# Value products in runs of two steps, and the softmax sums inverted on a compact tile, in a fused attention and expert kernel

## The chip, the cores and the metric

One Trainium2 chip, one of its cores. The metric is the device time of the whole program in microseconds (us), median of several runs. The text names TensorE (PE in the rows), VectorE (DVE), ScalarE (ACT), GpSimd (POOL) and SyncE (SP, which here only issues transfers).

## The reference

Sixteen items, each a row of 1101 tokens (1024 image patches and 77 text tokens) with 128 features, go through an embedding, a normalisation, one attention layer with 8 heads of 64, a residual, a second normalisation and a small mixture of experts. What the change touches is the attention:

```
scores = jnp.einsum('bhsk,bhtk->bhst', q, k) / jnp.sqrt(jnp.asarray(K, x.dtype))
probs = jax.nn.softmax(scores, axis=-1)
o = jnp.einsum('bhst,bhtk->bhsk', probs, v)
concated = jnp.transpose(o, (0, 2, 1, 3)).reshape(B, S, H * K)
return jnp.einsum('bse,ed->bsd', concated, head_kernel)
```

All data is float32, and the outputs too.

## The kernel before, in words

An item is cut into 108 **steps**: 4 pairs of heads, times 3 chunks of 368 (the last 366) query columns, times 9 key tiles of 128 (the last 77) rows. A step s is (p, c, t), and the nine steps of one (p, c) are here called a block; q counts the blocks of an item from 0 to 11. In step s:

- TensorE makes the scores of both heads of the pair, transposed, keys by queries, two matmuls a head (`score`, L759 and L761), into three rotating PSUM banks (`SB = 3`).
- ScalarE takes the exponential of each (L867) into one of three buffers of `probs` (`NP = 3`, buffer s % 3). The row maximum that keeps it in range was put into an extra row of the queries beforehand, by transfers (`maxrow`, L1200 and L1202).
- GpSimd adds the probabilities up over the nine key tiles into `sums` (L1151 and L1155), two buffers, one for even and one for odd blocks.
- TensorE multiplies the values of step s - 1 with their probabilities (`weigh`, L778) into the one bank `o_ps`, accumulated over the nine steps of a block. Each head uses 64 columns of the array, head 0 the lower, head 1 the upper half. The profile shows a float32 product as two records, so one call of `weigh` is four records of L778.

After a block: ScalarE copies `o_ps` into `heads_t` (L855). Two steps into the next block, TensorE sums `sums` over the partitions with a matrix of ones, in two halves of 64 columns again (the unit `sum`, L686), ScalarE copies that out (L826), VectorE inverts it in four pieces of 92 columns (`divide`, L991), one piece a step, and multiplies `heads_t` with it in the fifth (L997).

Between score and weigh of a step, and behind weigh, TensorE does **units** of other work, which go through four PSUM banks called `work`: projections of the next pair (`qk`, L669), the values (`v`, L662), raw scores of which VectorE takes the row maximum (`max`, L675, reduced by L925), and the experts of the item before (L718, L723, L734). A function `plan` decides ahead which unit stands in which step: by a table of loads (tens of ns on TensorE, VectorE, ScalarE), it puts some at fixed steps and fills the rest so that the steps are evenly loaded. Half of a step's units stand ahead of `weigh`, half behind. All engines run the same list of steps in order, so what an engine waits for holds up everything behind it in its own list. Items 1 to 14 are a loop on the chip; item 0 and item 15 are written out; the experts of item 15 follow as an epilogue without attention.

The two lines that set ScalarE's pace beside the scores are

```
wait(act, probs_used, ALL * b + s - NP + 1)
wait(act, sums_done, (NT - 1) * PAIRS * NC * b + summed(s - NP))
```

that is, a buffer of `probs` is written again when TensorE has weighed it and GpSimd has added it.

## Time and profile before

| | |
|---|---|
| median of 3 runs | 5209.72 us (5208.44 to 5212.94) |
| span of the profiled execution | 5214.6 us |
| busy share: TensorE matmul | 95% |
| busy share: VectorE | 73% |
| busy share: ScalarE | 51% |
| busy share: GpSimd | 54% |
| mean granted TensorE clock | 0.980 |
| length of one item in the loop | 318.10 us (from 1961.33 to 2279.43) |

The profiled execution is given by its span, which is 4.9 us (0.1%) over the median of the runs. Matmul records overlap: a record of 0.33 us follows the one before at a distance of 0.17 us, so it is the distance between starts, not the busy share, that says what a matmul costs.

### The profile page before, as it was taken

What the parts mean: (1) busy time and instruction counts of PE and PEld (TensorE: products, weight loads), DVE (VectorE), ACT (ScalarE), POOL (GpSimd) and SP (SyncE); (2) the same over time, 40 slices, a digit from 0 to 9 for tenths busy, and PEclk for the clock granted to TensorE, in tenths of its full rate; (3) what the DMA queues carried; (4) which work ended last, traced back from release to release, by engine and by line L of the source; (5) the groups of instructions that cost most, each with busy time, mean ns of one, the idle gap of its engine ahead of it and who ended that gap; (6) DMA issues with size and microseconds to landing.
All of it is one profiled execution on the core that took longest, in us unless ns stands there. A gap on an engine that the chain in (4) does not pass through costs nothing. (4 is left out here: it accounts for less than half of the span.)

```text
span 5214.6 us, 92843 instructions
## 1 busy us (share of the span) xinstructions
PE 4965.0 (95%) x25829; PEld 3227.2 (62%) x25829; DVE 3832.6 (73%) x8495; ACT 2665.8 (51%) x6408; POOL 2796.0 (54%) x1611
## 2 busy tenths in 40 slices
PE   5999999999999999999999999999999999999997
PEld 3556666666566666666666666666666656666666
DVE  5667768677776777777777776777867777677765
ACT  2664555555544545545455455455455554554542
POOL 0665555555555555555555555555555555555652
PEclk7999999999999999999999999999999999999998
DMA  1000000000000000000000000000000000000000
GB/s 39 6 10 7 6 16 6 11 7 6 16 6 10 7 10 11 6 11 11 10 6 6 10 11 11 7 6 16 6 11 7 6 16 6 10 6 10 6 1 14
DMA packets 43025, 49.54 MB, mean 10 GB/s; under 512 B 26256, under 2 KB 34311, under 8 KB 42503
## 3 DMA queue, kind: packets, MB, share of 16 engines
q1 hardware_dynamic: 42503, 43.12, 2.7%
q8 instruction: 262, 4.29, 0.4%
q14 instruction: 260, 2.13, 0.1%
HBM read 23.45 MB, written 19.09 MB: 8 GB/s over the span
## 5 line engine op out<-in xcount | busy, mean ns | idle before, releaser
L1155 POOL TENSOR_TENSOR sums<-sums,probs 128x736 f32<-128x736 f32 (+3 forms) x1344 | 2384.6, 1774 | 1278.0 <-ACT probs L867 1262.6
L867 ACT ACTIVATE probs<-scores 128x368 f32<-128x368 f32 (+3 forms) x3456 | 1460.1, 474 | 1922.0 <-PE scores L761 1814.5
L925 DVE TENSOR_REDUCE part_max<-work 128x1 f32<-128x368 f32 (+3 forms) x3456 | 1657.3, 527 | 310.1 <-PE work L675 288.3
L778 PE MATMUL o_ps<-probs,values 128*64 128x368 f32 (+1 forms) x6912 | 1455.7, 500 | 0.0
L759 PE MATMUL scores<-q_a,k_a 128*128 128x368 f32 (+3 forms) x3456 | 1170.2, 339 | 61.1 <-issue 41.5
L761 PE MATMUL scores<-q_b,k_b 128*128 128x368 f32 (+3 forms) x3456 | 1146.4, 332 | 0.0
L675 PE MATMUL work<-k_a,q_a 128*128 128x368 f32 (+3 forms) x3456 | 1089.6, 378 | 48.0 <-DVE part_max L925 24.4
L675 PEld LDWEIGHTS work<-k_a,q_a 128*128 128x128 f32 (+1 forms) x3456 | 578.3, 184 | 777.4 <-issue 624.1
L1151 POOL TENSOR_TENSOR sums<-probs 128x736 f32<-128x736 f32 (+1 forms) x192 | 343.6, 1789 | 863.5 <-ACT probs L867 861.5
L759 PEld LDWEIGHTS scores<-q_a,k_a 128*128 128x128 f32 (+1 forms) x3456 | 639.5, 185 | 83.8 <-issue 33.2
L761 PEld LDWEIGHTS scores<-q_b,k_b 128*128 128x128 f32 (+1 forms) x3456 | 641.3, 186 | 53.0 <-issue 33.7
L778 PEld LDWEIGHTS o_ps<-probs,values 128*64 128x64 f32 (+1 forms) x6912 | 349.5, 135 | 412.6 <-issue 327.3
L969 DVE SCALAR_TENSOR_TENSOR h_out<-work,comb,h_out 128x128 f32<-128x128 f32 x1152 | 404.1, 351 | 268.1 <-PE work L734 236.0
L991 DVE RECIPROCAL sums<-sums 128x92 f32<-128x92 f32 (+1 forms) x768 | 543.1, 713 | 12.8 <-ACT sums L826 11.7
L915 DVE TENSOR_TENSOR k_b<-work,k_a 64x368 fp32r<-64x368 f32 (+1 forms) x384 | 204.5, 533 | 375.8 <-ACT k_a L822 373.9
L918 DVE TENSOR_TENSOR q_a<-work,q_b 64x368 fp32r<-64x368 f32 (+1 forms) x384 | 207.0, 539 | 158.5 <-ACT q_b L822 153.2
L734 PE MATMUL work<-down_hi,hid_hi 128*128 128x512 f32 x576 | 237.6, 413 | 0.4 <-DVE q_a L918 0.4
L734 PE MATMUL work<-down_hi,hid_lo 128*128 128x512 f32 x576 | 231.0, 401 | 0.0
L734 PE MATMUL work<-down_lo,hid_hi 128*128 128x512 f32 x576 | 230.8, 401 | 0.0
L813 ACT COPY values<-work 128x256 f32<-128x256 f32 x288 | 107.6, 374 | 206.0 <-PE work L662 205.6
L820 ACT CAST k_a<-work 64x368 fp32r<-64x368 f32 (+1 forms) x384 | 177.2, 461 | 36.8 <-PE work L669 31.1
L820 ACT CAST q_a<-work 64x368 fp32r<-64x368 f32 (+1 forms) x384 | 176.2, 459 | 29.3 <-PE work L669 24.4
(186 smaller groups left out, 5039.6 us busy)
## 6 DMA issues: line engine op xcount, KB each, us to landing
resid_rows<-h_in SPq DMA_DIRECT2D x16, 576.0 KB, 2.8
h_out<-resid_rows SPq DMA_DIRECT2D x16, 576.0 KB, 4.1
h_in<-in_pe_table_dram SPq DMA_DIRECT2D x16, 512.0 KB
out_dram<-h_out SPq DMA_DIRECT2D x16, 512.0 KB
q_b<-max_rows SPq DMA_DIRECT2D x128, 4.0 KB
q_b<-max_rows SPq DMA_DIRECT2D x128, 0.3 KB
counts<-in_x_dram SPq DMA_DIRECT2D x16, 116.0 KB, 3.0
out_raw<-n_expert_out_weight_dram SPq DMA_DIRECT2D x1, 1024.0 KB
```

Of the source, the lines that this page charges most:

```text
L675: mm = nc.tensor.matmul(w[0:n, 0:cw], q_a[p % 2][i][:, j * P:j * P + n], k_a[p % 2][i][:, c0:c0 + cw], start=True, stop=True)
L734: mm = nc.tensor.matmul(w, h[:, k2, cols], wt[:, k2, g * EG * D:(g + 1) * EG * D], start=(n == 0), stop=(n == len(ops) - 1))
L759: nc.tensor.matmul(o, k_a[p % 2][i][:, t * P:t * P + n], q_a[p % 2][i][:, c0:c0 + cw], start=True, stop=False)
L761: nc.tensor.matmul(o, k_b[p % 2][i][:, t * P:t * P + n], q_b[p % 2][i][:, c0:c0 + cw], start=False, stop=True).then_inc(scores_ready, 1)
L778: mm = nc.tensor.matmul(o_ps[64 * i:64 * i + 64, 0:cw], values[0:n, t, h * DH:(h + 1) * DH], probs[0:n, s % NP, i, 0:cw], start=(t == 0), ...
L820: nc.scalar.copy(a[p % 2][i][0:64, c0:c0 + cw], src)
L867: nc.scalar.activation(probs[0:n, s % NP, i, 0:cw], scores[0:n, h % SB, 0:cw], ACT.Exp, scale=DH ** -0.5).then_inc(probs_ready, 1)
L925: nc.vector.tensor_reduce(part_max[0:n, i * NT + j, c:c + 1], w[0:n, 0:keys], AX.X, ALU.max).then_inc(drained[k], 1)
L969: ins = nc.vector.scalar_tensor_tensor(out=o, in0=w[:, e * D:(e + 1) * D], scalar=comb[:, t, g * EG + e:g * EG + e + 1], in1=o, op0=ALU.mu ...
L991: nc.vector.reciprocal(inverse[:, cols], inverse[:, cols]).then_inc(s_chain, 1)
L1151: nc.gpsimd.tensor_tensor(acc, probs[:, (s - 1) % NP, :, 0:cw], probs[:, s % NP, :, 0:cw], ALU.add).then_inc(sums_done, 1)
L1155: nc.gpsimd.tensor_tensor(acc, acc, probs[0:n, s % NP, :, 0:cw], ALU.add).then_inc(sums_done, 1)
```

## The change

Five things.

1. `weigh` is called in bursts. The nine steps of a block are grouped 2, 2, 2, 2, 1; the products of a group stand in the step behind it, so at t = 2, 4, 6, 8 (two steps each) and at t = 0 of the next block (the one left over). Steps t = 1, 3, 5, 7 have none.
2. `probs` keeps three buffers with another rule: the first step of a group takes buffer 0 or 1 in turn, the second always buffer 2. ScalarE's two waits go by that rule (`held`).
3. The unit `sum` stands in the step t = 2 as before (in the last block's case at step 2 of the next item, before at step 1), now directly behind the burst.
4. The inverse: the row of sums of each head goes by two transfers from one partition into a compact tile `inv_cols` of 92 partitions by 8 columns; VectorE inverts that in one instruction two steps after the sum; one transfer stores it to DRAM and two bring it back, each spread over 64 partitions.
5. GpSimd multiplies `heads_t` with it, at t = 0 of the second block after (step 0 and step 7 of the next item for the last two blocks).

The planner's loads change with it (a step 66 for the scores, and in a step with a burst 25 more and 62 for each product), so other units move too.

```
+GROUPS = (2, 2, 2, 2, 1)
+MOST = max(GROUPS)
+NP = 2 * MOST - 1
+SUM_AT = 2
+INVERT, SCALE_LAST = 2, 7
+RW = 8
-STEP = (130, 0, 70)
+SCORE = (66, 0, 70)
+EXCURSION, WEIGH = 25, 62
...
+def slot(s):
+    n, _, _, position = group_of(s)
+    return n % 2 * (MOST - 1) + position if position < MOST - 1 else NP - 1
...
+def held(s):
+    return next(back for back in range(1, ALL) if slot((s - back) % ALL) == slot(s))
...
         def step(seg, it, b, s):
             if seg.attn:
                 p, c, t = cut(s)
-                wait(act, probs_used, ALL * b + s - NP + 1)
-                if not isinstance(b, int) or b > 0 or s >= NP:
-                    wait(act, sums_done, (NT - 1) * PAIRS * NC * b + summed(s - NP))
+                back = held(s)
+                wait(act, probs_used, ALL * b + s - back + 1)
+                if not isinstance(b, int) or b > 0 or s >= back:
+                    wait(act, sums_done, (NT - 1) * PAIRS * NC * b + summed(s - back))
...
+        def invert(b, q):
+            dve.wait_ge(cols_loaded, 32 * (item_of(b, q) + 1))
+            nc.vector.reciprocal(inv_cols[:], inv_cols[:]).then_inc(cols_inverted, 1)
...
+        def scale(b, q):
+            c0, cw = CHUNKS[q % NC]
+            o = heads_t[:, q // NC, c0:c0 + cw]
+            pool.wait_ge(inverse_loaded[q % 2], 32 * (PAIRS * NC // 2 * b + q // 2 + 1))
+            pool.wait_ge(heads_out, PAIRS * NC * b + q + 1)
+            nc.gpsimd.tensor_tensor(o, sums[:, q % 2, 0, 0:cw], o, ALU.mult).then_inc(heads_scaled, 1)
...
+                elif u[0] == "sum":
+                    wait_then(wait_drained, sp, seg, it, u)
+                    for i in range(2):
+                        row = sums[64 * i:64 * i + 1, u[1] % 2, 0, :]
+                        half = slice(i * CHUNK // RW, (i + 1) * CHUNK // RW)
+                        sp.dma_start(inv_cols[half, :], row.rearrange("p (a n) -> p a n", n=RW)).then_inc(cols_loaded, 16)
+            for u in seg.at[s - INVERT] if s >= INVERT else []:
+                if u[0] == "sum":
+                    n = item_of(b, u[1])
+                    wait_then(sp.wait_ge, cols_inverted, n + 1)
+                    sp.dma_start(inv_dram[u[1] % 2].rearrange("(a n) -> a n", n=RW), inv_cols[:]).then_inc(cols_stored, 16)
+                    wait_then(sp.wait_ge, cols_stored, 16 * (n + 1))
+                    for i in range(2):
+                        row = inv_dram[u[1] % 2:u[1] % 2 + 1, i * CHUNK:(i + 1) * CHUNK]
+                        sp.dma_start(sums[64 * i:64 * i + 64, u[1] % 2, 0, :], row.broadcast_to((DH, CHUNK))).then_inc(inverse_loaded[u[1] % 2], 16)
```

TensorE, in a quiet stretch of the loop (block 1 of the item, the step t = 6 of the kernel before, from its second head's scores): a step is the scores, a unit, the products of the step before, more units. `ISA` and `REGISTER_ALU` rows hold waits and their arithmetic; `x2` stands for the two heads.

```order
L598 REGISTER_ALU
L759 MATMUL scores<-q_a,k_a 128x368
L761 MATMUL scores<-q_b,k_b 128x368
L598 REGISTER_ALU
L675 MATMUL work<-k_a,q_a 128x366
L767 ISA
L778 MATMUL o_ps<-probs,values 64x368 x2
L598 REGISTER_ALU
L675 MATMUL work<-k_a,q_a 128x366 x2
L598 REGISTER_ALU
```

The same engine and block in the changed kernel, the step t = 6 (L813 and L815 are the scores, L729 the raw scores for the maxima, L832 the products):

```order
L813 MATMUL scores<-q_a,k_a 128x368
L815 MATMUL scores<-q_b,k_b 128x368
L648 REGISTER_ALU
L729 MATMUL work<-k_a,q_a 128x366
L821 ISA
L832 MATMUL o_ps<-probs,values 64x368 x2
L821 ISA
L832 MATMUL o_ps<-probs,values 64x368 x2
L729 MATMUL work<-k_a,q_a 128x366
L729 MATMUL work<-k_a,q_a 128x368
```

Two products now stand side by side, and the step ahead of this one has none. Over the loop body, the runs of matmuls in 64-column halves (products and sums, counted as one run where nothing full-width stands between) are 117 before and 60 after; in the item ahead of the loop 115 and 59, in the last item with its epilogue 114 and 60.

TensorE before, where a block's sum stands (L686, block 1 of the item): full-width work (L695, L675) stands between it and the products.

```order
L759 MATMUL scores<-q_a,k_a 128x368
L761 MATMUL scores<-q_b,k_b 128x368
L598 REGISTER_ALU
L683 REGISTER_ALU
L686 MATMUL work<-sums,ones 64x368 x2
L695 MATMUL work<-wo,heads_t 128x128 x4
L675 MATMUL work<-k_a,q_a 128x368
L767 ISA
L778 MATMUL o_ps<-probs,values 64x368 x2
```

TensorE after, such a place at the loop's start (L740 is the sum): it is the tail of the burst.

```order
L821 ISA
L648 REGISTER_ALU x2
L832 MATMUL o_ps<-probs,values 64x368 x2
L821 ISA
L832 MATMUL o_ps<-probs,values 64x368 x2
L737 ISA
L740 MATMUL work<-sums,ones 64x366 x2
```

So the sum opens no run of its own any more, in any block.

The queue of SyncE before, around the first `maxrow` of the loop, which stands three steps behind the sum of block 1 and four ahead of the pair that needs it:

```order
L598 ISA
L1200 DMA q_b<-max_rows 1x8x128
L1202 DMA q_b<-max_rows 1x13x6
L1200 DMA q_b<-max_rows 1x8x128
L1202 DMA q_b<-max_rows 1x13x6
L598 ISA
```

The queue of SyncE after, the same place (L1259 and L1261 are the `maxrow` transfers; ahead of L1272 it waits for VectorE's inverse, ahead of L1276 for the store to have landed):

```order
L1267 DMA inv_cols<-sums 46x1x8 x2
L1228 REGISTER_ALU
L1272 DMA inverse_rows<-inv_cols 92x8
L1228 REGISTER_ALU
L1276 DMA sums<-inverse_rows 64x368 x2
L648 REGISTER_ALU
L1259 DMA q_b<-max_rows 1x8x128
L1261 DMA q_b<-max_rows 1x13x6
L1259 DMA q_b<-max_rows 1x8x128
L1261 DMA q_b<-max_rows 1x13x6
```

The `maxrow` transfers now queue behind a store, the wait for it, and two loads.

## Rows read from the trace of the kernel before

**Rows 1.** The page: span, busy times and shares.

```profile
span 5214.6 us, 92843 instructions
PE 4965.0 (95%) x25829; PEld 3227.2 (62%) x25829; DVE 3832.6 (73%) x8495; ACT 2665.8 (51%) x6408; POOL 2796.0 (54%) x1611
```

**Rows 2.** Windows, an item: length, busy PE, PEld, DVE, ACT, POOL (instructions), clock, DMA, GB/s.

```profile
1961.33:2279.43 318.10, 306.76 (x1609) 199.31 (x1610) 238.66 (x525) 165.98 (x399) 174.34 (x100) 0.99 0.03 9
```

**Rows 3.** Timeline of TensorE: start us, length us, engine, line, count.

```profile
2007.72 0.33 PE L761 MATMUL scores<-q_b,k_b 128*128 128x368 f32 x1
2007.89 0.33 PE L675 MATMUL work<-k_a,q_a 128*128 128x366 f32 x1
2008.15 0.84 PE L778 MATMUL o_ps<-probs,values 128*64 128x368 f32 x4
2008.92 0.44 PE L675 MATMUL work<-k_a,q_a 128*128 128x366 f32 x1
2009.20 0.33 PE L759 MATMUL scores<-q_a,k_a 128*128 128x368 f32 x1
```

**Rows 4.** Timeline of TensorE where a sum and a product stand together.

```profile
2365.81 0.84 PE L686 MATMUL work<-sums,ones 128*64 128x366 f32 x4
2366.48 0.79 PE L778 MATMUL o_ps<-probs,values 128*64 128x368 f32 x4
2367.20 0.43 PE L669 MATMUL work<-yt_hi,wqk_hi 128*128 128x368 f32 x1
2367.47 0.33 PE L669 MATMUL work<-yt_lo,wqk_hi 128*128 128x368 f32 x1
```

**Rows 5.** Groups by line: busy us, mean ns, idle before and releasers.

```profile
L867 ACT ACTIVATE probs<-scores 128x368 f32<-128x368 f32 (+3 forms) x3456 | 1460.1, 474 | 1922.0 <-PE scores L761 1814.5 <-POOL sums L1155 72.1 <-issue 24.4
L1155 POOL TENSOR_TENSOR sums<-sums,probs 128x736 f32<-128x736 f32 (+3 forms) x1344 | 2384.6, 1774 | 1278.0 <-ACT probs L867 1262.6
L991 DVE RECIPROCAL sums<-sums 128x92 f32<-128x92 f32 (+1 forms) x768 | 543.1, 713 | 12.8 <-ACT sums L826 11.7
L1062 DVE RECIPROCAL den<-den 128x9 f32<-128x9 f32 x16 | 3.4, 215 | 0.6
L997 DVE TENSOR_TENSOR heads_t<-sums,heads_t 128x368 f32<-128x368 f32 (+1 forms) x192 | 182.2, 949 | 3.8
L820 ACT CAST k_a<-work 64x368 fp32r<-64x368 f32 (+1 forms) x384 | 177.2, 461 | 36.8 <-PE work L669 31.1
```

**Rows 6.** Timeline: the queue of SyncE, and the scores of the next pair.

```profile
2352.08 0.68 SPq L1200 DMA_DIRECT2D q_b<-max_rows  x1
...
2354.35 0.77 SPq L1202 DMA_DIRECT2D q_b<-max_rows  x1
2357.83 0.33 PE L759 MATMUL scores<-q_a,k_a 128*128 128x368 f32 x1
```

**Rows 7.** Timeline, and the page's list of transfers (KB, us to landing).

```profile
117.54 0.77 SPq L1202 DMA_DIRECT2D q_b<-max_rows  x1
119.41 0.68 PE L759 MATMUL scores<-q_a,k_a 128*128 128x368 f32 x1 [4.08 <-DMA q_b<-max_rows]
...
resid_rows<-h_in SPq DMA_DIRECT2D x16, 576.0 KB, 2.8
```

**Rows 8.** Timeline around GpSimd's root in step 13.

```profile
2009.50 1.81 POOL L1130 TENSOR_TENSOR rstd<-var,minus_half 128x9 f32<-128x9 f32 x1 [3.49 <-DVE var L1024]
...
2013.43 0.85 ACT L867 ACTIVATE probs<-scores 128x368 f32<-128x368 f32 x2 [2.85 <-POOL sums L1155]
```

**Rows 9.** Timeline: the start of an item in the loop.

```profile
2281.40 0.48 ACT L867 ACTIVATE probs<-scores 128x368 f32<-128x368 f32 x1 [3.71 <-issue]
```

**Rows 10.** Timeline of the epilogue's sum and scaling.

```profile
5122.25 0.84 PE L686 MATMUL work<-sums,ones 128*64 128x366 f32 x4 [2.52 <-POOL sums L1155]
5127.84 0.53 DVE L997 TENSOR_TENSOR heads_t<-sums,heads_t 128x366 f32<-128x366 f32 x1
```

**Rows 11.** Timeline: a multiplication on VectorE while GpSimd adds.

```profile
2273.93 1.96 DVE L997 TENSOR_TENSOR heads_t<-sums,heads_t 128x368 f32<-128x368 f32 x1
```

More of the change, by code:

```diff
@@ L106, in maxima, with group_of, burst @@
     return units, first_need
+def group_of(s):
+    t, start = s % NT, s - s % NT
+    for n, size in enumerate(GROUPS):
+        if t < size:
+            return s // NT * len(GROUPS) + n, start, size, t
+        t, start = t - size, start + size
+def burst(s):
+    _, start, _, position = group_of((s - 1) % ALL)
+    if position < group_of((s - 1) % ALL)[2] - 1:
+        return []
+    start -= ALL if s == 0 else 0
+    return list(range(start, s))
+def slot(s):
[3 more added lines that the diff above has]
+    return next(back for back in range(1, ALL) if slot((s - back) % ALL) == slot(s))
 def load(u):
@@ L114, in plan @@
     at = [[] for _ in range(ALL)]
-    used = [list(STEP) if attn else [0, 0, 0] for _ in range(ALL)]
+    used = [list(SCORE) if attn else [0, 0, 0] for _ in range(ALL)]
+    for s in range(ALL):
+        if attn and burst(s):
+            used[s][0] += EXCURSION + WEIGH * len(burst(s))
     def job(s, name):
@@ L199, in plan, with beside_weighing @@
         fill(units, WEIGHTS + 3, STORE - 2, EVEN_POST)
-    return at
+    return [beside_weighing(units) for units in at]
+def beside_weighing(units):
+    sums = [u for u in units if u[0] == "sum"]
+    others = [u for u in units if u[0] != "sum"]
+    n = len(units) // 2
+    return others[:n] + sums + others[n:]
 class Segment:
```

71 lines of the change are left out of this document (33 added, 38 removed).

## The prediction

> **What bounds the kernel now.** The busy shares come first: TensorE 95%, no other engine over 73% [rows 1]. That share is no proof, since matmul records overlap, so I read starts. In the timeline a full-width matmul of 368 columns follows the one before at 0.17 us (2007.72 to 2007.89) [rows 3]. I priced the list of one item in the loop that way, from such distances: 216 each of L759, L761 and L675, 72 of L669 at 0.166 us (119.5); L718, L734 and L662 at 0.174, 0.232 and 0.117 (43.9); smaller units 18.9; the 64-column matmuls as below (120 products and sums at 0.615, 117 runs at 0.357: 115.5 with rounding). The sum is 297.7 us, and an item takes 318.1 [rows 2]. So TensorE streams for 94% of the loop, and about 20 us an item are waits and half-clock stretches. A shorter list on TensorE shortens the program, as long as nobody else comes to set the pace.
>
> The groups by line say the same from the other side: ScalarE waited 1814.5 us for scores and only 72.1 for GpSimd's sums; GpSimd 1262.6 for ScalarE [rows 5].
>
> **What a run in half-width columns costs.** The last full-width matmul before the products starts at 2007.89, the products at 2008.15: 0.26 where 0.17 is usual. The next full-width one starts 0.77 later (2008.92), and its successor 0.28 after that [rows 3]. So a run of one product takes 0.26 + 0.77 + 0.28 less two usual distances of 0.17, 0.98 us. Where a sum and a product stand together, both go in 1.39 (2365.81 to 2367.20), and the successor follows at 0.27 [rows 4]; the gap ahead is again 0.26, and there are 62 such places after scores, nearly all alike. The second member adds 0.62 where a run of its own adds 0.98: each run that goes away gives back 0.36 us (0.357 by the middle values of all such places: 0.154 inside, 0.095 ahead, 0.108 behind).
>
> The Trainium skill says in "TensorEngine Tiling (Array Packing)", section Key Properties, that changing the tiling mode, not just the tile, drains TensorE. By that rule too the price hangs on the number of changes of width, and the trace agrees with its 0.26 and 0.28 at the two edges.
>
> **The change, part by part.**
>
> *Bursts and sums.* Runs in the loop fall from 117 to 60 an item, in the first item from 115 to 59, in the last with epilogue from 114 to 60: 57 x 14 + 56 + 54 = 908. At 0.357 that is 324 us. The products themselves stay (0.62 each). That two products in a row cost what a sum and a product do is not shown: they add into the same bank `o_ps`, the sum goes to another. Bounds: 0 if a product behind a product costs 0.98 again, 0.36 if like the sum. Inside one product its own two passes already add to one bank without harm (four records in 0.77), so I take 0.36.
>
> *VectorE.* 768 pieces at 0.713 and 192 multiplications at 0.949 go, 725 us; 192 compact inverses come. No row has 92 x 8, the nearest is 128 x 9 at 0.215: 0.2 each, 40 us. TensorE waits for VectorE now and then, a gain of 0 to 2 us an item; I take 1.
>
> *GpSimd.* 192 multiplications of 368 columns; the nearest row is 1.774 us for 736, so between 0.9 and 1.8; I take 0.9. A block then costs it 8 x 1.77 + 0.9 = 15.1 us, TensorE's block (297.7 - 20.3) / 12 = 23.1. Hidden; the shortest pair of steps in the new plan is 3.4 us on TensorE against 3.5 for two additions, which is no lasting lag.
>
> *The chain of the inverse.* Copy of the sums 0.5 (a cast of the same width takes 0.46 [rows 5]), two issues 1.4, landing, VectorE 0.2, store issue 0.7, landing, two load issues 1.4, landing. An issue takes 0.66 to 0.79 [rows 6]. A landing is 1.1 us after the issue's end for a small transfer (118.31 to 119.41), and 2.8 after the issue of a large one [rows 7]. That makes 4.2 + 3 x 1.1 to 3 x 2.1, 7.5 to 10.5 us, plus what VectorE comes late. GpSimd asks for it six steps later, some 15 us. Hidden. VectorE asks for the tile after two steps, at least 3.9 us by the plan, and it lands 3.0 to 4.0 after the sum: hidden or nearly; behind a late one stand VectorE's maxima, which free TensorE's banks. I give 0.5 us an item. [...]
>
> *The queue of SyncE.* Here a wait can come. The inverse of block 1's sum is asked for at step 22, and `maxrow` stands at step 23. It queues behind store issue 0.7, landing 2, load issues 1.4, then needs its own 2.9 [rows 6] and 1.1 to 1.8 to land: about 9.2 us after step 22. TensorE is at the next pair after the four steps 23 to 26, 8.1 us in the new plan. Before, the slack was 2357.83 - 2355.12 = 2.7 less the landing [rows 6]. I charge 1.5 us for this pair and 1 for the start of the item, where the store of the output also stands in the queue; the other two pairs have 10 us and more ahead of them.
>
> *Two buffers back.* The second step of a group now needs the buffer of the step two back, not three. It bites where GpSimd is late. In step 13 it waited 3.49 us for the variance, took 1.81 for the root, and ScalarE's next exponential but two came 2.85 us late [rows 8], without a stop of TensorE. In the new plan the exponential of step 16 needs one addition more (1.77), while TensorE needs it in the same burst: 1.5 us an item.
>
> *ScalarE in the first six steps of a pair.* It has exponentials of 0.85 and four casts of 0.46 a step there [rows 5], 17.7 to 20.7 us, and TensorE before 15.6 to 17.7, after 14.4 to 16.5. What TensorE gains there is partly given back: 1 us an item. The start of an item, where ScalarE comes 3.71 us late and TensorE waits for it [rows 9], stays.
>
> *Epilogue.* The scaling ended 6.1 us after the sum started (5122.25 to 5128.37) [rows 10], under projections that don't need it. The new chain is some 11 us with GpSimd's 0.9, and nothing covers the rest: 5 us.
>
> *Sum.* 324 - 16 x (0.5 + 2.5 + 1.5 + 1 - 1 for VectorE's relief), 72 us, - 5 = 247. From the span of 5214.6 that is 4968, and less the 4.9 us by which the span lies over the median, 4963. I say 4963.
>
> **The rivals.**
>
> *All of it arrives* (0.15). New waits are swallowed by the 20 us an item that TensorE idles anyhow, and VectorE's relief takes more of them away: 5210 - 324, 4886, give or take 12. For it: VectorE drops from 239 to about 196 busy us an item. Against it: the idle stretches lie at the item's start and at pauses, not where the new waits fall.
>
> *Pacing eats half* (0.20). ScalarE, GpSimd and the transfers share three buffers with less slack, and uneven steps (by the same prices 1.2 us for the shortest without a burst, up to 4 with one) leave TensorE waiting once a block: 12 x 0.8 = 10 us an item more, 5120. For it: rows 8 show how near the edge one late addition is. Against: a pair of steps is long enough for one exponential, one addition and one exponential (0.85 + 1.77 + 0.85 = 3.5 against 3.4 at the shortest, 5.1 on average).
>
> *VectorE is held up by GpSimd.* A multiplication of 0.53 alone [rows 10] took 1.96 while additions ran [rows 11]. More work on GpSimd, more such holds; but the one instruction of this kind that came every block is the one that goes away, so this stays inside the forecast. The Trainium skill ("SBUF — State Buffer", section on the two separate sides) calls this an exclusive lock on a shared port pair, held for a whole instruction; the 1.96 agrees. By that rule 0.9 us more a block could stop VectorE, 11 us an item of an engine that then idles some 100.
>
> *Slower* (0.04). The chain of the inverse is longer than the six steps until GpSimd asks. GpSimd then stops ahead of the additions, those hold the buffers, and TensorE stops. It bites from 15 us of chain and costs 192 us per us beyond; from 16.3 us it has eaten the gain, at 19 us the time is 4963 + 192 x 4 = 5731. It would take transfers of 4 to 5 us each; none in the trace needs more than 2.8.
>
> *The change doesn't do it* (0.06). A product behind a product drains as before: only the 60-odd sums that join are gained (9 an item, 144 x 0.36 = 52 us), against 77 of new waits: 5235. That counts as slower; with lighter waits it is within 0.2%.
>
> **The numbers.** Forecast 0.55, all 0.15, half 0.20, nothing 0.06, slower 0.04. Gains over 0.2% (10 us, about what a measurement of this kernel can tell from no change): 0.55 + 0.15 + 0.20 = 0.90, and a little of the fifth: 0.91; same 0.03; slower 0.06. The range holds the forecast with the bounds of its waits (1.5 to 9 us an item: 4915 to 5040), the upper half of the first rival and part of the second: 4890 to 5070.
>
> **What would show it.** Right: 57 runs in half width less in an item, an item of 302 us, products of a burst 0.62 us apart, GpSimd's multiplication at 0.9 with no wait ahead of it, and small waits of TensorE at the start of pair 1 (for `max_rows`) and in step 17. Wrong: products 0.98 apart; GpSimd waiting for `inverse_rows`; VectorE waiting for `inv_cols` by more than a us a block; ScalarE's wait for `sums` far over 72 us with TensorE idle behind it.

## The result, and the profile after

The changed kernel takes 5268.99 us (median of 4 runs, 5256.67 to 5274.85), the kernel before in the same session 5210.89 (5208.44 to 5212.94): a ratio of 1.0107, 95% interval 1.0092 to 1.0121. It is 1.1% slower, 306 us from the forecast, outside its range, and on the side that had 0.06.

The head of the page of the changed kernel, against [rows 1]:

```profile
span 5262.3 us, 94506 instructions
PE 4774.0 (91%) x25829; PEld 3366.3 (64%) x25829; DVE 3256.8 (62%) x7727; ACT 2673.5 (51%) x6408; POOL 2950.3 (56%) x1803
```

TensorE has 191 us less to do and VectorE 576, and the program is 48 us longer. The time saved came back as idle time, and more. The mechanism that was to save is there. Timeline of TensorE in a quiet stretch, a burst with a sum and a burst alone (against [rows 3, 4]):

```profile
2331.26 0.41 PE L729 MATMUL work<-k_a,q_a 128*128 128x368 f32 x1
2331.60 1.46 PE L832 MATMUL o_ps<-probs,values 128*64 128x368 f32 x8
2332.89 0.79 PE L740 MATMUL work<-sums,ones 128*64 128x368 f32 x4
2333.61 0.60 PE L729 MATMUL work<-k_a,q_a 128*128 128x368 f32 x2
...
2336.93 0.33 PE L815 MATMUL scores<-q_b,k_b 128*128 128x368 f32 x1
2337.20 1.46 PE L832 MATMUL o_ps<-probs,values 128*64 128x368 f32 x8
2338.58 0.44 PE L813 MATMUL scores<-q_a,k_a 128*128 128x368 f32 x1
2338.86 0.33 PE L815 MATMUL scores<-q_b,k_b 128*128 128x368 f32 x1
```

Two products take 1.38 (2337.20 to 2338.58), as a sum and a product did in [rows 4]; with the sum it is 2.01 (2331.60 to 2333.61). The gap ahead is still 0.27, the one behind 0.28. A second product costs 0.62 and no second pair of gaps.

The groups by line, against [rows 5], and VectorE's compact inverse and GpSimd's multiplication:

```profile
L927 ACT ACTIVATE probs<-scores 128x368 f32<-128x368 f32 (+3 forms) x3456 | 1462.7, 474 | 1869.5 <-PE scores L815 1649.8 <-POOL sums L1214 182.2 <-POOL sums L1210 24.6
L1043 DVE RECIPROCAL inv_cols<-inv_cols 92x8 f32<-92x8 f32 x192 | 36.4, 190 | 7.3 <-DMA inv_cols<-sums 5.4
L1185 POOL TENSOR_TENSOR heads_t<-sums,heads_t 128x368 f32<-128x368 f32 (+1 forms) x192 | 190.6, 992 | 11.2 <-DMA sums<-inverse_rows 10.9
```

The instructions of the inverse path wait for next to nothing: 5.4 us for `inv_cols` and 10.9 for `inverse_rows` in the whole program (8.2 of it once, in the epilogue). The transfers as such are hidden.

The item, against [rows 2]: 324.14 us, where it had 319.72 at the same place of the program (the eighth item). Windows of that item, the six steps of each pair in which the next pair's projections (`qk`) are made: length, busy PE, PEld, DVE, ACT, POOL, clock, DMA, GB/s. The kernel before:

```profile
2279.43:2300.57 21.14, 18.15 (x89) 11.94 (x90) 8.31 (x16) 14.59 (x34) 7.25 (x6) 0.84 0.01 2
2357.83:2377.62 19.79, 17.64 (x95) 12.10 (x94) 14.40 (x34) 17.34 (x42) 8.44 (x6) 1.00 0.15 36
2442.86:2461.85 18.99, 18.97 (x102) 13.10 (x101) 15.31 (x29) 15.80 (x38) 9.65 (x6) 1.00 0.00 1
2521.82:2541.22 19.40, 18.71 (x101) 12.85 (x100) 12.77 (x25) 17.90 (x44) 8.55 (x5) 1.00 0.00 1
```

The changed kernel:

```profile
2292.36:2315.64 23.28, 18.41 (x88) 13.19 (x89) 7.85 (x17) 14.47 (x34) 8.16 (x6) 0.78 0.07 24
2372.86:2397.34 24.48, 18.22 (x95) 13.25 (x95) 13.92 (x29) 18.89 (x45) 10.55 (x7) 0.95 0.14 35
2457.47:2478.11 20.64, 18.28 (x92) 13.27 (x92) 13.89 (x26) 14.99 (x37) 8.05 (x6) 0.92 0.01 1
2536.66:2561.77 25.11, 20.17 (x102) 14.93 (x101) 12.46 (x25) 18.27 (x43) 9.68 (x6) 0.93 0.02 7
```

The 24 projection steps grew from 79.3 to 93.5 us; the other 84 shrank from 240.4 (2279.43 to 2599.15, less 79.3) to 230.6 (2292.36 to 2616.50, less 93.5). In the second and fourth window TensorE and ScalarE are each idle for 5 to 7 us, so it is no engine's amount of work that makes them long: they wait for each other. The chain of who waits for whom is in TensorE's list of waits (us in total, times, longest), of the changed kernel:

```profile
PE work L772 <- DVE q_a L977: 78.2, 42, 2.2
PE scores L813 <- DMA q_b<-max_rows: 47.7, 30, 4.1
PE work L729 <- DVE k_b L974: 35.0, 32, 1.9
PE work L723 <- DVE q_a L977: 26.2, 30, 1.0
PE work L788 <- DVE q_a L977: 25.5, 25, 1.6
```

The largest, 42 times, is three times an item in 14 items of the loop: in steps 30, 32 and 82. Of the wait in the last row, at L788 (`expert`), 21.9 us are in step 86. L772 is the unit `up` of the experts. It does not read `q_a`: it waits for the bank of `work` that VectorE empties when it makes `q_a`. The plan says why it is those steps. Units of some projection steps, before and now:

```
         before                     changed
step 30  qk max up                  qk max max up up
step 32  qk up                      qk max max up up
step 57  qk max max                 qk max max shared expert
step 82  qk up up                   qk v v up up
step 86  qk expert                  qk max max shared expert
```

There are four banks, and they go round. A fifth unit in a step needs the bank that the `qk` of the same step has just filled. Timeline of step 82 (weight loads and other rows left out):

```profile
2539.99 0.33 PE L723 MATMUL work<-yt_hi,wqk_hi 128*128 128x368 f32 x1
...
2541.52 0.38 PE L716 MATMUL work<-wv_hi,yt_hi 128*128 128x256 f32 x1 [0.51 <-DVE k_b L974]
2541.70 0.85 ACT L927 ACTIVATE probs<-scores 128x368 f32<-128x368 f32 x2
...
2542.10 0.44 PE L772 MATMUL work<-flat_hi,up_hi 128*128 128x384 f32 x1
...
2542.42 0.45 ACT L879 CAST q_a<-work 64x368 fp32r<-64x368 f32 x1
...
2543.63 0.46 ACT L881 CAST q_b<-work 64x368 fp32r<-64x368 f32 x1
...
2544.12 0.54 DVE L977 TENSOR_TENSOR q_a<-work,q_b 64x368 fp32r<-64x368 f32 x1 [0.32 <-ACT q_b L881]
...
2544.72 0.45 PE L772 MATMUL work<-flat_hi,up_hi 128*128 128x384 f32 x1 [1.83 <-DVE q_a L977]
...
2545.57 0.51 PE L813 MATMUL scores<-q_a,k_a 128*128 128x368 f32 x1
...
2545.80 0.49 ACT L899 ACTIVATE hid<-work 128x384 f32<-128x384 f32 x1 [1.04 <-PE work L772]
2545.87 0.51 PE L815 MATMUL scores<-q_b,k_b 128*128 128x368 f32 x1
```

The `qk` of the step starts at 2539.99. Behind it in ScalarE's list stand the two exponentials (2541.70), then four casts of 0.46 from that bank (2542.42 to 2544.09), and behind them VectorE's subtraction (to 2544.66). Only then may the fifth unit start (2544.72), and the next step's scores stand behind it (2545.57): 6.2 us for a step, with ScalarE idle for 1.04 us at its end.

Step 57 also has five units, but loses its time at the third. There the second `max` needs the bank of the `qk` of step 56, and VectorE comes late to empty it, because a cast ahead of it in its list takes 1.96 us while GpSimd adds (the same cast takes 0.35 in step 35):

```profile
2465.56 1.96 DVE L1048 CAST flat_hi<-normed 128x384 fp32r<-128x384 f32 x1
2469.17 0.43 PE L729 MATMUL work<-k_a,q_a 128*128 128x368 f32 x1 [1.86 <-DVE k_b L974]
```

This wait comes to 27.1 us in the program. The kernel before has none of it, though its `max` needs the same bank and the cast takes 1.67 us in the same step; the steps around it hold other units. The fifth unit of step 57 waits 3.6 us in all, those of 30, 32, 82 and 86 together 100.1.

### The profile page after: what moved, and what is told of

It reads as the page before. It is cut to its first block, busy times and chain, and to the rows that moved or that the text cites. A ratio compares the mean times of both kernels' runs of the same rounds, so it can differ in the third digit from the quotient of the medians.

```text
span 5262.3 us, 94506 instructions
## 1 busy us (share of the span) xinstructions
PE 4774.0 (91%) x25829; PEld 3366.3 (64%) x25829; DVE 3256.8 (62%) x7727; ACT 2673.5 (51%) x6408; POOL 2950.3 (56%) x1803
## 4 chain that ended last, share of the span: by engine, by line
PE 69%; ACT 10%; DVE 7%; issue 7%; DMA 2%; SPq 2%; POOL 2%; ACTq 0%; DVEq 0%; POOLq 0%
PE o_ps L832 20%; PE work L729 11%; PE scores L813 8%; PE work L788 8%; PE scores L815 8%; PE work L772 3%; PE work L723 3%; ACT probs L927 2%; DVE part_max L984 2%; PE work L749 2%; ACT q_b L881 2%; ACT q_a L879 2%; PE work L740 2%; ACT k_a L881 1%; ACT k_a L879 1%
## 5 line engine op out<-in xcount | busy, mean ns | idle before, releaser
L984 DVE TENSOR_REDUCE part_max<-work 128x1 f32<-128x368 f32 (+3 forms) x3456 | 1676.7, 532 | 581.3 <-PE work L729 566.4
L832 PE MATMUL o_ps<-probs,values 128*64 128x368 f32 (+1 forms) x6912 | 1304.7, 494 | 0.0
L813 PE MATMUL scores<-q_a,k_a 128*128 128x368 f32 (+3 forms) x3456 | 1186.8, 343 | 82.2 <-DMA q_b<-max_rows 47.7
L815 PE MATMUL scores<-q_b,k_b 128*128 128x368 f32 (+3 forms) x3456 | 1161.3, 336 | 45.1 <-issue 45.1
L729 PE MATMUL work<-k_a,q_a 128*128 128x368 f32 (+3 forms) x3456 | 990.3, 364 | 73.5 <-DVE k_b L974 35.0
L729 PEld LDWEIGHTS work<-k_a,q_a 128*128 128x128 f32 (+1 forms) x3456 | 578.3, 185 | 482.5 <-issue 344.4
L813 PEld LDWEIGHTS scores<-q_a,k_a 128*128 128x128 f32 (+1 forms) x3456 | 651.0, 188 | 217.8 <-issue 114.0
L832 PEld LDWEIGHTS o_ps<-probs,values 128*64 128x64 f32 (+1 forms) x6912 | 416.9, 138 | 498.4 <-issue 409.2
L815 PEld LDWEIGHTS scores<-q_b,k_b 128*128 128x128 f32 (+1 forms) x3456 | 651.1, 188 | 69.0 <-issue 49.2
L788 PE MATMUL work<-down_hi,hid_hi 128*128 128x512 f32 x576 | 245.3, 426 | 32.7 <-DVE q_a L977 25.5
L772 PE MATMUL work<-flat_hi,up_hi 128*128 128x384 f32 x384 | 146.6, 382 | 102.5 <-DVE q_a L977 78.2
L885 ACT COPY sums<-work 128x368 f32<-128x368 f32 (+1 forms) x192 | 89.6, 467 | 283.3 <-PE work L740 280.6
L788 PE MATMUL work<-down_hi,hid_lo 128*128 128x512 f32 x576 | 232.3, 403 | 0.0
L788 PE MATMUL work<-down_lo,hid_hi 128*128 128x512 f32 x576 | 232.2, 403 | 0.0
L1185 POOL TENSOR_TENSOR heads_t<-sums,heads_t 128x368 f32<-128x368 f32 (+1 forms) x192 | 190.6, 992 | 11.2 <-DMA sums<-inverse_rows 10.9
```

The lines of the kernel that those rows point to most:

```text
L729: mm = nc.tensor.matmul(w[0:n, 0:cw], q_a[p % 2][i][:, j * P:j * P + n], k_a[p % 2][i][:, c0:c0 + cw], start=True, stop=True)
L772: mm = nc.tensor.matmul(w[:, 0:GW], wt[:, path, m, :], y[:], start=(n == 0), stop=(n == 2))
L788: mm = nc.tensor.matmul(w, h[:, k2, cols], wt[:, k2, g * EG * D:(g + 1) * EG * D], start=(n == 0), stop=(n == len(ops) - 1))
L813: nc.tensor.matmul(o, k_a[p % 2][i][:, t * P:t * P + n], q_a[p % 2][i][:, c0:c0 + cw], start=True, stop=False)
L815: nc.tensor.matmul(o, k_b[p % 2][i][:, t * P:t * P + n], q_b[p % 2][i][:, c0:c0 + cw], start=False, stop=True).then_inc(scores_ready, 1)
L832: mm = nc.tensor.matmul(o_ps[64 * i:64 * i + 64, 0:cw], values[0:n, t, h * DH:(h + 1) * DH], probs[0:n, slot(s), i, 0:cw], start=(t == 0), ...
```

## The experiments

All against the kernel before in the same session (5209.25 to 5213.72). The last two columns name the projection steps of an item with five and with four units.

| kernel | median us | ratio, 95% interval | five | four |
|---|---|---|---|---|
| changed | 5268.99 | 1.0107 (1.0092 to 1.0121) | 30 32 57 82 86 | 4 28 84 |
| bursts_only | 5175.35 | 0.9923 (0.9905 to 0.9941) | 28 | 32 57 82 |
| inverse_only | 5206.4 | 0.9991 (0.9981 to 1.0001) | none | 4 32 57 59 84 86 |
| max_first | 5245.07 | 1.0066 (1.0045 to 1.0086) | as changed | as changed |
| level | 5104.98 | 0.9791 (0.9774 to 0.9809) | none | 4 32 57 59 84 86 |
| half | 5126.21 | 0.9837 (0.982 to 0.9853) | none | 4 28 30 32 57 59 84 86 |
| level_max | 5085.95 | 0.9764 (0.9747 to 0.978) | none | as level |
| level_old_inverse | 5144.47 | 0.9874 (0.9857 to 0.989) | none | none |
| level_buf4 | 5052.81 | 0.9697 (0.9681 to 0.9713) | none | as level |
| qk_heavy | 5174.43 | 0.9926 (0.991 to 0.9943) | none | 4 32 86 |
| uneven_rest | 5086.32 | 0.9761 (0.9745 to 0.9777) | none | 4 32 57 |
| root_late | 5107.37 | 0.9799 (0.9782 to 0.9815) | none | as level |
| root_qk | 5132.79 | 0.9846 (0.9829 to 0.9862) | none | 4 |
| cap4 | 5180.85 | 0.9935 (0.9918 to 0.9951) | none | 4 28 30 32 57 59 82 84 86 |
| level_five | 5194.97 | 0.9971 (0.9956 to 0.9985) | 32 57 84 86 | 4 |
| rest_max | 5062.52 | 0.9713 (0.9697 to 0.973) | none | 4 32 57 |
| rest_cap3_max | 5046.96 | 0.9682 (0.9666 to 0.9698) | none | none |
| cap3 | 5111.14 | 0.9804 (0.9788 to 0.9821) | none | none |

**Which part of the change?** bursts_only is the changed kernel with the inverse as before, in four pieces on VectorE; inverse_only is the kernel before with the transfers, the compact inverse and GpSimd's multiplication.

```
bursts_only:   -INVERT, SCALE_LAST = 2, 7      +DIV = 4
               -JOB "invert": 8                +JOB "invert": 63, "scale": 45
               -dve: invert(b, u[1])           +dve: divide(seg, it, b, u[1], part)
               -sp: dma inv_cols, inverse_rows, sums;  pool: scale(b, q - 2)
inverse_only:  the same lines the other way round, on the kernel before
(in words; the planner's JOB is VectorE's load of these instructions)
```

> The changed kernel with the inverse as it was before: four reciprocals and a multiplication on VectorE, no transfers, no multiplication on GpSimd. Theory A (the loss comes with the bursts: heavy units pile up in the steps without products, scores get only one step of lead, TensorE and ScalarE take turns in waiting, and the clock drops in the new waits): the time stays near the changed kernel's 5269, between 5230 and 5300, and the waits at steps 30 to 33, 57, 82 and 86 of an item stay. Theory B (the loss comes with the inverse's way over the transfer queue and GpSimd): the 324 us of the fewer runs come through, near 4900 to 4960.

> The kernel before with only the new inverse (compact tile, transfers, multiplication on GpSimd), products one a step, plan by the old loads. Theory A: close to before, 5190 to 5235, with up to 45 us of waits for max_rows as in the changed kernel, and VectorE's relief against it. Theory B: 5400 and more, since the transfers would cost some 380 us with nothing to set against them.

The inverse alone changes nothing that can be measured (5206.4 beside 5212.76). The bursts alone gain 37 us, between what the two theories had (5230 to 5300, and 4900 to 4960). Together they lose. Neither part is at fault alone, and each also moves the planner's units, since both change its loads.

**The planner's table.** level gives every step the same load for scores and products, as before the change; half goes half way.

```
level:  -SCORE = (66, 0, 70)                                          +SCORE = (130, 0, 70)
        -        if attn and burst(s):
        -            used[s][0] += EXCURSION + WEIGH * len(burst(s))
        +        pass
half:   -SCORE = (66, 0, 70)          +SCORE = (98, 0, 70)
        -EXCURSION, WEIGH = 25, 62    +EXCURSION, WEIGH = 12, 31
```

> The changed kernel with the planner's old load of a step (130 in every step, nothing extra for bursts), so units are spread evenly over steps with and without products. Theory A in its form 'uneven units are to blame': the steps without products get shorter and those with products longer, the experts no longer stand ahead of the scores in steps 57, 82 and 86; 5080 to 5200. If it is the bursts themselves that take the lead of the scores away, whatever stands between: 5230 to 5300. Theory B: no change, 5269.

> The changed kernel with a planner's table half way between its own and the flat one: 98 in every step, in a step with a burst 12 more and 31 for each product. If the unevenness of the units is what costs 164 us, the time lies between 5105 and 5269, some 5150 to 5220. If it was one unlucky place of a unit, it lies at one of the two ends.

Three numbers are worth 164 us: 5104.98, 2.1% faster than before. The new table, which follows TensorE's load more closely, is the worse one. Half way gives back nearly all (5126, where 5150 to 5220 was expected), which does not fit a loss in proportion to the unevenness, but fits the number of steps with five units: five in the changed kernel, none in either of these.

**The queue of SyncE.** max_first lets the loads of the inverse go one step later, so that the `max_rows` transfers pass them; level_max does it to level.

```
-                    wait_then(sp.wait_ge, cols_stored, 16 * (n + 1))
+            for u in seg.at[s - INVERT - 1] if s >= INVERT + 1 else []:
+                if u[0] == "sum":
+                    n = item_of(b, u[1])
+                    wait_then(sp.wait_ge, cols_stored, 16 * (n + 1))
```

> The changed kernel, but SyncE brings the inverse back one step later, so that the transfers of max_rows are issued ahead of the wait for the store. TensorE's waits for max_rows (47.7 us over the program against 5.8 before) fall to under 10: 5215 to 5240 by theory A (up to 42 us, and some of the clock). Theory B in its form 'the queue of SyncE is the whole loss': under 5100.

> Flat table and max_rows ahead of the inverse's return, both. If they are separate causes their gains add: 5105 less about 24, 5070 to 5090. If the waits for max_rows only took the place of others: 5105.

Both gain: 24 us and 19. TensorE's wait for `max_rows` falls from 47.7 us in 30 places (41.8 in level) to one at the program's start, so about half of the length of these waits was worth time. In max_first:

```profile
PE scores L813 <- DMA q_b<-max_rows: 4.1, 1, 4.1
```

**Does VectorE's relief pay?** level_old_inverse is bursts_only with level's table (the edits are those shown).

> Flat table, bursts, and the inverse on VectorE as before the change. The transfers cost waits for max_rows (42 us of 5105); VectorE's 700 us of reciprocals and multiplications come back. If the transfers are the greater cost: 5060 to 5090. If VectorE's relief is: 5110 to 5140.

It takes 5144.47, 39 us more than level. So with a flat table the new inverse is a gain, with the new table it comes with a loss of 94 (5175 to 5269), and there it goes with five crowded steps in place of one. Where the old inverse costs most is step 17 of the item, told next: it takes 7.1 us there and 4.6 in level, 39 us over the program. The other steps of the two profiled runs differ both ways: 5.3 us an item less in the projection steps, 6.9 more in the rest.

**The buffers.** level_buf4 is level_max with four buffers of `probs` in plain rotation. To have room it leaves out the low part of the projection weights (`wqk_hi` is used in its place; the matmuls stay).

```
-NP = 2 * MOST - 1      +NP = 4
-    return n % 2 * (MOST - 1) + position if position < MOST - 1 else NP - 1      +    return s % NP
```

> As level_max, with four buffers of probabilities in plain rotation (a step's buffer is free when the step four back is weighed and added) in place of three. To make room it leaves out the low part of the query and key weights (the high part is read twice, same instructions in the loop). If the three buffers with the second step's two-back rule cost time (step 17's 1.7 us an item, and ScalarE's waits for sums): 20 to 50 us under level_max. If not: the same within 10.

33 us less. The run tells time only, since its projections are not the true ones. ScalarE's wait for GpSimd's sums, first in level_max, then in level_buf4:

```profile
ACT probs L926 <- POOL sums L1213: 135.4, 53, 4.2
```

```profile
ACT probs L922 <- POOL sums L1209: 88.6, 46, 2.0
```

The place that loses it is step 17, of 2.4 us before the change, 4.6 in the changed kernel and level_max, and 2.9 in level_buf4. GpSimd waits for the variance, takes the root, and its additions start late behind it; ScalarE needs the buffer that they read, and TensorE the exponential. Timeline of the changed kernel there:

```profile
2339.69 1.81 POOL L1175 TENSOR_TENSOR rstd<-var,minus_half 128x9 f32<-128x9 f32 x1 [2.32 <-DVE var L1070]
...
2341.74 3.58 POOL L1214 TENSOR_TENSOR sums<-sums,probs 128x736 f32<-128x736 f32 x2
...
2345.43 0.85 ACT L927 ACTIVATE probs<-scores 128x368 f32<-128x368 f32 x2 [4.18 <-POOL sums L1214]
2345.96 0.39 PE L813 MATMUL scores<-q_a,k_a 128*77 128x368 f32 x1 [1.49 <-ACT probs L927]
```

root_late tries to cure it without a buffer, and root_qk adds the heavier load of a projection unit that is told next:

```
root_late (on level_max):  -if seg.post and s == STATS:       +if seg.post and s == STATS + 2:
                           -if seg.prep and s == EMBED + 4:   +if seg.prep and s == EMBED + 6:
root_qk (on root_late):    -LOAD "qk": (48, 95, 130)          +LOAD "qk": (112, 95, 130)
```

> The flat table with the transfers of max_rows first (5086), and GpSimd's two roots an item issued two steps later, behind the additions of those steps. If the wait in step 17 comes from the root, which holds the additions while GpSimd waits for the variance, it goes: 1.7 us an item, 27 us, 5060, near the run with four buffers of probs (5053). Rival: the root only moves, and the wait with it, or what hangs on the root comes late: 5080 to 5100.

> As the run before, with the projection unit's load at 112. If lighter projection steps help beside a flat table too, 5040, 20 us less than with 48. Rival: with the flat table there is little left to take there, and the other steps become fuller: within 10 us of the run with 48.

Both were worse than level_max (5107 and 5133 beside 5086). The wait in steps 15 to 17 only fell from 1.8 to 1.2 us an item, and what hangs on the second root came 2.5 us an item later in step 65. Two steps later is too late for the root; no other place was tried. And fewer units in the projection steps are no good by themselves: root_qk is 25 us slower than root_late.

**Where is the table's loss?** qk_heavy keeps the changed kernel's table and makes only projection steps lighter; uneven_rest makes them flat and leaves the new table everywhere else.

```
qk_heavy:     -LOAD "qk": (48, 95, 130)     +LOAD "qk": (112, 95, 130)
uneven_rest:  -        if attn and burst(s):
              +        if attn and s % (NC * NT) < 6:
              +            used[s][0] += 76
              +        elif attn and burst(s):
```

> The changed kernel, only the planner's load of a projection unit (qk) raised from 48 to 112, so that 12 instead of 23 other units of the experts and values stand in its 24 steps of an item; elsewhere the table's alternation of full and empty steps stays. Theory A, the loss sits in the steps of the projections, where heavy units stand between one score and the next behind a bank that ScalarE and VectorE give back late: about 5150, between 5105 (the flat table) and 5180. Rival B, the loss comes from the alternation of steps with and without products wherever it stands: 5240 to 5270, as the changed kernel.

> The mirror of the run with the heavier projection unit: the changed kernel, with the flat load in the six projection steps of each pair (76 added there, nothing for the products), and the new table's alternation in all others. Theory A: most of the gain of the flat table arrives, 5110 to 5150. Rival B: three quarters of the steps still alternate, so 5210 to 5250.

uneven_rest is decisive: with the new table in 84 of 108 steps it takes 5086.32, even less than level. Its 84 other steps take 1.7 us an item more than level's, with two more units in them, and its projection steps 3.1 less. So full and empty steps in turn cost next to nothing outside the projection steps. qk_heavy gains 95 of 164 us: 18 us an item less in the projection steps than the changed kernel, and 12 more in the others, where the units have gone.

**What in those steps?** cap4 and cap3 keep the changed kernel and its whole table and only forbid a fifth (a fourth) unit in a projection step; level_five puts four such fifth units into level.

```
cap4, cap3:  +MAX_UNITS = 4        (cap3: 3)
             +        def full(s, places):
             +            return any(x[0] == "qk" for x in at[s]) and len(at[s]) + sum(n == s for n, _ in places) >= MAX_UNITS
             -                while s <= last and (u == PAUSE or weighted(used[s]) + backlog >= level):
             +                while s <= last and (u == PAUSE or weighted(used[s]) + backlog >= level or full(s, places)):
level_five:  +FIFTH = (32, 57, 84, 86)
             +    for s in FIFTH if post and attn else []:
             +        n = next(n for n in range(s + 1, ALL) if any(u[0] in ("up", "shared", "expert") for u in at[n]))
             +        u = next(u for u in at[n] if u[0] in ("up", "shared", "expert"))
             +        at[n].remove(u)
             +        at[s].append(u)
```

> The changed kernel with its own table of loads; only the planner may not give a projection step a fifth unit, so single units leave the steps 30, 32, 57, 82 and 86 for later ones and nothing else is meant to change. Theory C, the fifth unit of such a step needs the work bank of that step's own qk unit, which stands behind two exponentials, four casts and two subtractions, and holds up the next scores: the waits of the five steps (15.8 us an item in the changed kernel) fall to some 5, 10 us an item, 5090 to 5130. Rival B2, the uneven filling of the projection steps as a whole costs it: it hardly changes there, so 5220 to 5270.

> The mirror: the flat table (5105), and in the steps 32, 57, 84 and 86, which have four units, the next unit of the experts is drawn forward as a fifth; four units an item move by one to three steps. Theory C: each such step costs about 2.5 us more, 10 us an item: 5220 to 5280. Rival B2: four units more or less early cost 0 to 2 us an item: 5100 to 5140.

> The changed kernel and its table, with at most three units in a projection step, so that it has no fourth either (the cap of four gave 5181). If the rest of the loss is the projection unit of the next step waiting for the bank of this step's (72 waits of 66.5 us in all in the capped kernel, in places behind a step of four units): 5115 to 5145. Rival, the rest is the uneven load of the other steps once units are pushed there: 5165 to 5185.

Taking the fifth units away gives 88 us, putting four in costs 90. Both fell between my two theories: the fifth unit is about half of it. But level_five is not a clean mirror. In three of its places the fifth unit waits for the bank of `q_a`, 28.7 us in all. In step 84 it is a `shared`, drawn forward to just behind the `up` whose result it reads, and its largest wait is for that result:

```profile
2523.54 0.54 DVE L982 TENSOR_TENSOR q_a<-work,q_b 64x368 fp32r<-64x368 f32 x1 [0.32 <-ACT q_b L886]
2525.02 0.54 DVE L1021 SCALAR_TENSOR_TENSOR hid<-hid,work 128x384 f32<-128x384 f32 x1
2525.61 1.23 PE L782 MATMUL work<-down_sh,hid 128*128 128x128 f32 x4 [2.88 <-DVE hid L1021]
```

The bank was free at 2524.08, `hid` at 2525.56. These waits are 40.4 us in 14 items. About half of each, some 20 of the 90 us, is the wait for the result and not for the bank; that is an estimate from the two times. cap4, which takes units away, has no such place. In cap4 a neighbour of the wait is left, the projection unit of the next step (L727), which after a step of four units needs the bank of this step's:

```profile
PE work L727 <- DVE q_a L981: 66.5, 72, 1.2
```

cap3 has no step of four either, and no such wait; its largest for a bank is

```profile
PE work L733 <- DVE k_b L978: 61.7, 102, 1.6
```

and it takes 5111.14: 158 of the 164 us, with the new table untouched. Its second and fourth window, which were 24.48 and 25.11 in the changed kernel:

```profile
2307.06:2323.71 16.65, 15.31 (x84) 10.67 (x83) 9.52 (x17) 15.32 (x38) 9.24 (x6) 1.00 0.16 40
2463.79:2480.71 16.92, 15.84 (x86) 11.34 (x86) 9.93 (x18) 15.59 (x39) 8.95 (x6) 1.00 0.01 1
```

**The best.** rest_max is uneven_rest with `max_rows` first, rest_cap3_max adds the cap of three (edits as shown).

> The run with the flat load in the projection steps alone (5086), with the transfers of max_rows ahead of the loads of the inverse. Those were worth 24 us in the changed kernel and 19 with the flat table: 5065. Rival: the waits overlap by now, 5080 to 5086.

> As the run before, and no projection step gets a fourth unit either. If the fourth unit of a step, which needs the bank of the unit ahead of the qk or of the qk unit of the step before, costs as well, 5045 to 5060. Rival: nothing left there, 5060 to 5075.

5062.52 and 5046.96, the fastest kernel here that computes everything: 3.2% below the kernel before, 4.2% below the changed one.

The same in one table, per item (mean of 12 items of the loop). For each two neighbouring matmul records of TensorE of the same two shapes I took the tenth percentile of the distance between their starts as the one without a wait; what lies above it is summed as "waits", half-clock stretches among it. The split between waits and the rest hangs on how pairs are grouped (by line too, or by the record ahead too). By other groupings the rise from before to changed is 20 to 23 us, and that in the projection steps 19 to 20; in cap3 the rise is 8 to 12 us, where this table has 10.

```
               item   waits   of it in the 24 projection steps   in the other 84
before         318.8   22.2     9.1                               13.2
changed        322.8   44.6    28.9                               15.7
cap4           317.1   39.6    20.3                               19.3
cap3           311.8   32.2    13.7                               18.5
level          311.6   31.6    16.6                               15.0
level_five     318.3   36.9    23.1                               13.8
uneven_rest    310.2   31.8    15.1                               16.7
rest_cap3_max  307.7   27.5    12.3                               15.2
```

## Why the prediction was wrong

The step that failed is the one headed "ScalarE in the first six steps of a pair", with its 1 us an item, and with it the sum, which charged 4.5 us an item for all new waits, net of VectorE's relief. The item without its waits fell from 296.6 to 278.2 (318.8 - 22.2, 322.8 - 44.6), 18.4 us where 20.3 were forecast; the waits rose by 22.4, and 19.8 of that is in those six steps of each pair, where 1 was charged. I weighed these steps by their totals, 17.7 to 20.7 us of ScalarE against 14.4 to 16.5 of TensorE, and by totals they still looked like a small loss. What each step held, and in which bank, I did not look at, though the diff said that other units move and the order of the changed kernel showed where to. What stood in its place is a wait of TensorE for a bank of `work`: 100.1 us of it for the fifth units alone. The miss of 306 us is made up so: 158 the crowded projection steps (5269 to 5111 by cap3), and 148 between 5111 and 4963.

The 148, by the item: the distances without waits fell by 17.0 us in cap3 (296.6 to 279.6) and not by 20.3, 3.3 x 16 = 53 us; the waits rose by 10.0 (22.2 to 32.2) and not by the sum's 4.5, 5.5 x 16 = 88. These two are rough, by the grouping of pairs told above. Point by point:

- *Bursts and sums*: right. 0.62 for the second product; a product behind a product is no dearer than behind a sum, so the rival in which the runs give nothing back is out, although the time came out on its side. The count was one off: the trace has 116 runs an item before and 60 after, since the sum in step 1 stood beside a product already. That makes 894 runs and 319 us, 5 less than forecast.
- *VectorE*: 768 pieces and 192 multiplications gone, the compact inverse 0.19 (0.2 forecast). Its relief is worth more than the 16 us credited: 39 us net of all that the transfers cost (level_old_inverse to level), as long as it doesn't come with crowded steps. The two plans differ in their units too, so this is the worth of the whole edit.
- *GpSimd*: 0.99 for a multiplication, 0.9 forecast; hidden.
- *VectorE held up by GpSimd*: it is there, and it was said to stay inside the forecast. VectorE's busy time fell by 576 us, not by the 689 that went (725 less 36 for the compact inverse); the others took 113 more. What grew starts while GpSimd is at work: `flat_lo` (L1049) takes 0.56 us when it starts beside an idle GpSimd (all 48 before, 32 now) and 2.02 when not (16 now). Where it shows on TensorE is the cast ahead of step 57's `max`; in rest_cap3_max that cast falls into step 55, and the wait in step 57 is gone, though other units moved there too.
- *The chain of the inverse*: hidden, waits of 5.4 and 10.9 us. In the epilogue, from the copy of the sums (5169.16) to GpSimd's start (5177.24), it takes 8.1 us, within the 7.5 to 10.5. The slower rival was wrong in its mechanism: the chain of the inverse is not longer than six steps. (Its remark that no transfer needs more than 2.8 us is a misreading: the page of the kernel before has `h_out<-resid_rows` with 4.1.)
- *The queue of SyncE*: the wait is where it was put, 47.7 us less the 4.1 at the start, 2.7 us an item against 2.5; 27.7 us of it at the start of the item and 14.1 at pair 1, so the larger share is the other way round. (The terms of its sum for pair 1 make 8.1 to 8.8, not 9.2.) Taking it away gave 19 to 24 us, not 40.
- *Two buffers back*: 1.7 us an item in step 17 against 1.5; a fourth buffer gave 33 us. ScalarE's wait for `sums`, a sign of being wrong if it went far over 72 us, rose to 206.8 (182.2 and 24.6). It isn't what the 158 hang on: cap3 has 217.4 for the longer additions alone, and is the faster by 158.
- *The start of an item*: taken to stay; waits in its first six steps rose from 5.5 to 8.7 us in the changed kernel, and cap3 still has 7.9, some 38 us of the 148.
- *Epilogue*: GpSimd waited 8.2 us for the rows, and TensorE 2.8 for it; 5 was charged.
- *Pacing eats half* had the right size (5120) for what is left once no projection step is crowded (5111 in cap3, waits 10.0 us an item above before), for a partly wrong reason. Full and empty steps in turn, which I named as its cause, cost at most 1.7 us an item where there is no `qk` (uneven_rest). Of what the start of the item leaves of the 88 us, 22 are the wait in step 57, still there in cap3. The rest stays open, as does why the distances fell less than forecast.

So the plan of the projection steps is shown to be the cause of the 158 us, by runs that change nothing but the plan (cap4, cap3). That the bank is the reason is read from the trace and not tried by itself: a bank drained sooner, or a fifth bank, with the plan left as it is, should give the same. All runs moved the units and not the drain.

The Trainium skill's rule on tiling modes ("TensorEngine Tiling (Array Packing)", Key Properties) held in the trace after as before: the price is at the edges of a run (0.27 and 0.28) and not in its members.

## What to carry to other kernels

When a change re-weights a scheduler, compare the two plans step by step, not in totals: here three numbers of a table turned a gain of 2% into a loss of 1%. With n rotating banks, count the units between two uses of the slowest-drained one; an (n+1)th unit in a step puts the whole drain (here two exponentials, four casts and a subtraction) on the path of the critical engine, and everything queued behind it pays. A model of one engine's load that is more exact is no better plan, if the limit at that place is a buffer.

## What the runs showed of the hardware

In step 82 a wait of TensorE cost more than its length. After the wait of 1.83 us the granted clock fell to its lower level. Windows of the changed kernel, up to the fifth unit and behind its start:

```profile
2539.33:2545.00 5.67, 3.33 (x18) 2.64 (x18) 3.48 (x7) 5.31 (x14) 1.74 (x1) 1.00 0.00 0
2545.00:2547.80 2.80, 2.80 (x10) 2.43 (x9) 0.81 (x2) 1.45 (x3) 0.11 (x1) 0.51 0.00 0
```

At 0.51 (1.2 of 2.4 GHz) the scores follow each other at 0.30 (2545.57 to 2545.87), elsewhere at 0.17. TensorE had been busy 3.33 of the 5.67 us before. The mean granted clock over the program is 0.980 before, 0.966 in the changed kernel, 0.977 in cap3 and 0.976 in level: a plan with fewer long waits gets back part of the clock too. The stretches at the lower level add up to 213 us before, 364 in the changed kernel and 234 in cap3. In the changed kernel one begins in step 82 in all 14 items of the loop, in step 57 in 10 and in step 32 in 8; in steps 30 and 86, whose fifth units wait some 1.6 us, none does. TensorE was busy for 287 of the 364 us and for 171 of the 234. An estimate from this and the two distances: (287 - 171) x 0.13 / 0.30, some 50 of the 158 us are the clock.

A VectorE instruction from one tile to another can take several times as long when it starts while GpSimd works: the cast `flat_hi` 0.35 us alone and 1.84 in the mean of the 30 that so start in the changed kernel, `counts` 0.19 and 0.95, `flat_lo` 0.56 and 2.02. So a unit moved in the plan can lengthen an instruction that it has nothing to do with.

Two half-width members of a run cost the same whether they add to one bank or to two: two products (one bank) take 1.39 us from their start to the next full-width matmul (middle value of 576 places in the changed kernel), a sum and a product (two banks) 1.38 (64 places before).
